# Two-order graph network kernel: record scatters over 125 partitions without a bounds check, in place of 128 with one

## The reference, cut to what matters

```
x = x + mlp((1 + eps) * xn + segment_sum(edge_weight * xn[src], dst))   # layer 0, graph
x = x + expert_ffn(xn)                                                  # layer 0, 8 experts
x = x + typed_attention(xn, src, dst, edge_attr)                        # layer 1, graph
x = x + slice_attention(xn)                                             # layer 1
```

## Time and profile before

| | us |
|---|---|
| median of 3 runs | 4742.64 |
| lowest, highest | 4734.96, 4743.93 |
| span of the profiled execution | 4777.7 |
| POOL busy in it | 2723.8 |
| PE busy in it | 2872.2 |

### The profile page before, as it was taken

One profiled execution on the slowest core, in us unless ns is written; L12 is line 12 of the kernel. 1 busy time (PEld: TensorE's weight loads), 2 busy tenths in 40 slices (PEclk: granted clock), 3 DMA queues, 4 the chain that ended last, 5 costly groups with the idle time before them and its releaser, 6 DMA issues.

```text
span 4777.7 us, 52094 instructions
## 1 busy us (share of the span) xinstructions
PE 2872.2 (60%) x13590; PEld 1938.9 (41%) x13692; DVE 2426.9 (51%) x4965; ACT 1720.4 (36%) x4345; POOL 2723.8 (57%) x2661
## 2 busy tenths in 40 slices
PE   3200025555533239367677777997777776997588
PEld 1000013333332126223444444887444444886445
DVE  7444444544421001433667677566677777566353
ACT  2232300000011002222455554786555554885451
POOL 5676756666645740466555554788555553555551
PEclk6555557767665569767777777999777777998799
DMA  4343356333414224267766667687777666665300
GB/s 143 113 172 126 143 111 231 89 89 91 98 57 165 97 89 148 68 200 212 216 199 208 200 200 184 177 213 184 205 202 209 201 202 166 160 173 149 110 1 27
DMA packets 767484, 720.00 MB, mean 151 GB/s; under 512 B 389089, under 2 KB 661163, under 8 KB 767068
## 3 DMA queue, kind: packets, MB, share of 16 engines
q1 hardware_dynamic: 645116, 399.08, 29.2%
q0 software_dynamic: 115136, 314.24, 22.4%
q10 hardware_dynamic: 6944, 3.34, 0.2%
HBM read 482.09 MB, written 243.22 MB: 152 GB/s over the span
## 4 chain that ended last, share of the span: by engine, by line
PE 22%; another core or an unknown queue 17%; DVE 16%; issue 12%; ACT 9%; DVEq 4%; POOL 2%; ACTq 2%; DMA 1%; SPq 1%; POOLq 0%
DVE META L1380 5%; DVE BIGR L605 3%; ACT AR L1674 3%; DVE AR L1400 3%; PE ps L1657 2%; PE ps L933 2%; PE ps L944 2%; ACT AR L1676 2%; DVE AR L596 2%; DVEq L1396 2%; PE ps L1480 1%; PE ps L1478 1%; ACTq L1675 1%; PE ps L1428 1%
## 5 line engine op out<-in xcount | busy, mean ns | idle before, releaser
L1349 POOL DMA_INDIRECT AR<-kv_tab,META x832 | 793.7, 954 | 620.8 <-DVE AR L1393 363.1
L1380 DVE TENSOR_REDUCE META<-ps 128x8 f32<-128x1024 f32 x416 | 508.5, 1223 | 186.3 <-remote 94.2
L493 POOL DMA_INDIRECT rec_dst<-AR,slot_e x400 | 403.3, 1008 | 229.1 <-issue 171.0
L625 PE MATMUL ps<-AR 128*128 128x256 f32 x832 | 318.2, 550 | 345.4 <-DVE AR L596 156.4
L579 POOL DMA_INDIRECT AR<-xn_tab,META x416 | 398.6, 958 | 206.8 <-issue 139.0
L1618 POOL TENSOR_TENSOR AR<-AR 128x896 f32<-128x896 f32 x208 | 351.4, 1689 | 246.1 <-ACT AR L1683 241.6
L1583 DVE TENSOR_TENSOR BIGR<-BIGR,ps 128x260 f32 x832 | 354.3, 426 | 217.4 <-PE ps L1657 131.1
L1478 PE MATMUL ps<-AR,identb 128*128 128x512 bf16 x832 | 403.8, 485 | 79.1 <-issue 55.2
L1657 PE MATMUL ps<-AR 128*128 128x260 f32 x1664 | 413.9, 392 | 2.1 <-POOL AR L1618 2.0
L625 PEld LDWEIGHTS ps<-AR 128*128 128x128 f32 x832 | 219.7, 277 | 445.1 <-issue 214.9
L1526 ACT ACTIVATE AR<-ps 12x512 bf16<-12x512 bf16 x208 | 122.1, 587 | 671.8 <-remote 469.9
(11 more groups left out here) (430 smaller groups left out, 5624.0 us busy)
## 6 DMA issues: line engine op xcount, KB each, us to landing
v_dst<-AR SPq DMA_DIRECT2D x104, 384.0 KB
AR<-v_dst SPq DMA_DIRECT2D x104, 384.0 KB
v_src<-AR SPq DMA_DIRECT2D x104, 384.0 KB
AR<-v_src SPq DMA_DIRECT2D x104, 384.0 KB
AR<-in_W_qvk SPq DMA_DIRECT2D x44, 608.0 KB
rec_raw<-AR SPq DMA_DIRECT2D x40, 640.0 KB
AR<-rec_dst SPq DMA_DIRECT2D x104, 192.0 KB
AR<-rec_src SPq DMA_DIRECT2D x104, 192.0 KB
```

Of the source, the lines that this page charges most:

```text
L493: pool.indirect_dma_start(rec_tab[0], bass.IndirectOffsetOnAxis(ap=slot_e[0][:, c * CC + k:c * CC + k + 1].bitcast(U32), axis=0), RD[s][0] ...
L625: ins = pe.matmul(l0_ps(s, u), OW[s][:, u, :], GA[s][:, u, :], start=True, stop=True)
L1349: pool.indirect_dma_start(KVR[s][:, u, 0:KV], None, kv_tab, bass.IndirectOffsetOnAxis(ap=META[o][:, g * U + u, 0:1].bitcast(U32), axis=0)) ...
L1380: ve.tensor_reduce(BMALL[o][:, g * U + 2 * half:g * U + 2 * half + 2, :].rearrange("p b h -> p (b h)"), PSA[:, 2048 + 1024 * half:3072 + 1 ...
```

## The change

```diff
--- before.py
+++ after.py
@@ -491,8 +491,8 @@
                 pool.nop(nofuse=True)
                 for k in range(CC):
                     pool.indirect_dma_start(
-                        rec_tab[0], bass.IndirectOffsetOnAxis(ap=slot_e[0][:, c * CC + k:c * CC + k + 1].bitcast(U32), axis=0),
-                        RD[s][0][:, k, :], None, bounds_check=NB * P - 1, oob_is_err=False,
+                        rec_tab[0], bass.IndirectOffsetOnAxis(ap=slot_e[0][0:EP, c * CC + k:c * CC + k + 1].bitcast(U32), axis=0),
+                        RD[s][0][0:EP, k, :], None,
                     ).then_inc(sem(f"rd_sent{s}"), 16)
 
         def scatter_src_pool(pool, c0, c1):
@@ -519,8 +519,8 @@
 
         def scatter_src(pool, c, k, buf):
             pool.indirect_dma_start(
-                rec_tab[1], bass.IndirectOffsetOnAxis(ap=slot_e[1][:, c * CC + k:c * CC + k + 1].bitcast(U32), axis=0),
-                buf[:, k * REC:(k + 1) * REC], None, bounds_check=NB * P - 1, oob_is_err=False,
+                rec_tab[1], bass.IndirectOffsetOnAxis(ap=slot_e[1][0:EP, c * CC + k:c * CC + k + 1].bitcast(U32), axis=0),
+                buf[0:EP, k * REC:(k + 1) * REC], None,
             ).then_inc(sem(f"r2_sent{c % 4}"), 16)
 
         META_EDGE = (0, 2) + tuple(range(8, NG + 1, 8))
```

## The result

The changed kernel takes 4540.44 us (median of 5 runs, 4536.16 to 4545.78) against 4743.93 us for the kernel before in the same comparison (4734.96 to 4745.17). The ratio is 0.958, with a 95% interval of 0.9564 to 0.9596: 4.2% or 203 us faster, where 0.4% was forecast. The profiled execution took 4545.78 us with a span of 4544.0.

What follows compares the result with a forecast made beforehand. No engine is full; POOL's scatters pace the embed stage and slow other engines in the MLP and expert stages. Gains of 8.7 + 1.4 + 4.7 + 0.4 = 15.2 us, scaled to 15.1, gave 4727.5 us; range 4712 to 4800.

Steps and rivals of the forecast that it cites:

- What bounds the kernel: Whole kernel: no engine full; POOL's scatters pace the embed stage, and other engines crawl beside them in MLP and expert stages.
- The three rows at nothing: Record scatters: dropping partitions 125 to 127 saves at most 0.009 us a scatter, taken as nothing.
- The factors 0.77 and 0.72: MLP and expert stages: share of each us of earlier crawl end that is saved, from PE's busy rates.
- The check: Record scatters at POOL: removing the bounds comparison saves 0.023 us each, taken from the gather of line 579.
- The register load: Ahead of scatters: hidden in the 0.30 us gap where fast; removing the slow ones gives 2.4 us in the expert stage.
- The slower rival: Record scatters: 125 rows lengthen generation by 0.09 us, net +0.07 us each, about 4787 us; chance 33%.
- Much faster: MLP and expert stages: the crawl goes away if check or register load caused it, about 4490 us; chance 6%.
- The embed stage: 77 to 662 us, POOL sets the pace: 400 scatters save 9.2 us, of which 8.7 us are left.
- the rival of the longer scatter: The slower rival under another name: a scatter lasts longer at POOL with 125 rows; chance 33%.
- The sum pass: First sum pass, last 100 scatters: 0 us gained, since PE is the limit and covers them.

## Why the prediction was wrong

**What bounds the kernel: read rightly, used wrongly.** The prediction found the slow pace and that the end of the scatters ends it. It concluded that the pace is "one of unbroken issuing, with or without a check", which the runs confirm: 128 rows are slow with and without it. What it did not ask is how long the break must be. Between 1.29 and 1.38 us of pitch the stages come mostly free, and the change moves the pitch across.

**The three rows at nothing: the step that failed.** "If time per row were the whole difference ... 0.009 us for three. I take nothing." With it the pitch stayed at 1.28 us in the sum, and PE's rate beside the scatters stayed a fifth and a quarter: 1.4 us were forecast for the MLP stage and 4.7 for the experts. Measured were +0.21 us a scatter, and 71 and 174 us gained in these stages. The price of rows was taken as linear, and it is not: without a check 112, 120, 126, 128 rows cost 936, 987, 984, 962 ns, 85 and 125 cost 1077 and 1190. The Trainium skill ("DMA: Bandwidth & Descriptors", section "Why a DMA increments its semaphore by 16 and not by 1") has the count of engines, the largest number up to 16 that divides the rows; the packet sizes agree with five for 125. It does not say that the generator is slower then; the runs put that at 0.21 us with a check (1190 against 978) and 0.23 without (1190 against 962). Why the generator takes longer is not shown. The factors 0.77 and 0.72 were also taken from PE's busy time; by its matmuls (58 in 96 us against 348 in 60, 120 in 241 against 651 in 186) they are 0.90 and 0.86, which would add about 1 us.

**The check: mis-sized.** 0.023 us a scatter were taken from the gather. The 128-row scatter without check is 0.016 us shorter, and the kernel's ratio is 0.9998 (0.9983 to 1.0012), so the interval just leaves out 15 us (0.9968). At 125 rows the check's price is 0.000. The register load, 2.4 us, is likewise lost in that interval.

**The slower rival: right mechanism, larger price, wrong sign.** It wanted generation to grow by 0.09 us; it grew by 0.23, net 0.21. In the embed stage that cost 26 us and not 400 times 0.21 = 84. POOL had idle time there that was not issue gap, 229.1 less 171.0 = 58 us, because the engines that fill its buffers were late (ACT line 465 with 34.0 us, the rest with no visible releaser). No longer slowed, they are not late any more: all of the 169.2 us after are issue gap, and DVE now waits 261.8 us for the scatters where it waited 85.3. On the chip without the slow pace this rival could be expected to rule. The changed kernel did not run there. From the three memsets, 173 us for 0.25 us on 700 scatters, 0.21 us on the same 700 would cost some 145 us, an estimate.

**"Much faster": right result, wrong cause, 6%.** Its terms were 74 us in the MLP stage and 170 in the expert stage; measured were 71 and 174. That the terms agree so well is in part luck: they were worked out with 1.25 us a scatter from PE's rates, and what came was POOL's waits less 80 and 180 times 0.21 us (70 and 173). The embed stage is off, a gain of 9 forecast and a loss of 26, and the 17 us after line 998 are in no term. Its 4490 us lie 50 under the result. It was tied to check and register load and so given little. The evidence against those was sound. The fault was to let the outcome stand or fall with one cause: by the earlier trace rows some 240 us were to be had from anything that ends the slow pace, and the rival of the longer scatter thins out POOL's issuing. The two were never put together.

**The sum pass** behaved as said: 0 for its 100 scatters, the later part within 3 us, though they too grew by 0.22 us (median 1226 ns in place of 1006).

## What to carry to other kernels

When the profile shows engines held to a slow pace beside POOL's indirect transfers, treat what POOL does between two transfers as a knob of its own: two memsets behind each transfer, of which the first fits into the gap, gave 5.3% here, more than the change. Don't shorten or lengthen a row count without looking at its divisors; 125 rows cost a fifth more than 128. And measure such a thing on more than one chip: the same edit was 3.8% faster on one and 4.4% slower on another, so a pause like this is right only where the slow pace exists.

## What the runs showed of the hardware

- A scatter's duration at POOL by row count (512 B rows, ns at the median): 112 rows 936 ns, 120 rows 987, 126 rows 984, 128 rows 962, 85 rows 1077, 125 rows 1190, all without a check; 128 rows with one 978. The software queue's packets in the whole kernel are 115136 with 128, 120 or 112 rows, 127936 with 126 and 153536 with 125, so with 126 and 125 rows 16 and 48 more per scatter.
- A bounds check costs POOL 0.012 to 0.016 us at 128 rows (978 or 974 against 962 ns) and nothing at 125.
- One kernel took 3960 us on one chip and 4745 to 4781 on four others. On the slower four the other engines are held back while 112- to 128-row scatters follow each other at 1.24 to 1.29 us. Their starts then lie at multiples of about 0.70 us: DVE's statistics and PE's matmuls 2.80 us apart, POOL's register loads 691 ns long. Short bursts at full pace lie between: PE has 21 matmuls in 5.19 us from 1599.57 us on.
- What makes it so was not found. The DMA engines are busy for 0.35 of the time in the expert stretch, and four loads of instructions start in it. It is shown that 125 and 85 rows remove the slow pace, and that two or three memsets between scatters of 128 rows do; why is not.
